# A four-part network with three batches in flight: biases added by TensorE, x*sigmoid(x) as one ScalarE function, the last step of the norms and several copies on ScalarE, queries and keys turned together

## The reference, cut to what matters

```python
# block 1: state space model (16 states), then gated attention in chunks of 256 tokens
v  = silu(xn @ v_w.T + v_b);  mx = silu(s6(xn) + xn * D_p)
u, zr, hx = split(mx @ mx_w.T + mx_b)
u = sigmoid(u);  z, r = split(silu(zr))
q, k = z * gamma0 + beta0, z * gamma1 + beta1
h = silu(hx + (softmax(q @ k.T + bias + mask) @ v * r) @ h_w.T + h_b)
out = residual + u * (h - residual)
# block 2: silu(x @ wg.T) * (x @ wu.T) @ wd.T, hidden width 384
# block 3: causal attention, 16 heads of 8, biases on q, k, v and the output
# block 4: two layers of: shift tokens, q, k, v of 8 heads of 64, q and k to unit length,
#   scale, rotate (cos, sin); attention in windows of 64; x += o @ wo;
#   layernorm over features, * ln_g + ln_b; x += (a * gelu(g)) @ w2 + b2, hidden width 341
```

## Time and profile before

| | |
|---|---|
| median of 3 runs | 1905.69 us |
| the profiled execution | 1899.97 us |
| its span | 1898.2 us (1.8 us lie around it) |
| mean granted TensorE clock | 0.895 of full |
| busy: PE, DVE, ACT, POOL | 81%, 78%, 57%, 20% of the span |
| loads of a function table | 86 |

### The profile page before, as it was taken

The page is one execution under the profiler, slowest core; times in us unless marked ns, Lnnn a source line. Parts: engine busy times, 40 slices in busy tenths (PEclk is TensorE's granted clock), DMA queues, the critical chain, the costliest instruction groups (busy, mean ns, idle before and its releaser), DMA issues.

```text
span 1898.2 us, 30428 instructions
## 1 busy us (share of the span) xinstructions
PE 1530.9 (81%) x11540; PEld 843.3 (44%) x11540; DVE 1478.0 (78%) x2885; ACT 1082.9 (57%) x2536; POOL 381.4 (20%) x279
## 2 busy tenths in 40 slices
PE   3656688889987898877778898888857888999896
PEld 1113433544544555533344455435423453465574
DVE  6999875865489978598998858898699767566855
ACT  4325515437676677635664476377642663687783
POOL 0000000303025234100321214123002112143640
PEclk7678878879999999979899899799978897999999
DMA  6651304200023200415124002232053012000110
GB/s 246 232 169 43 68 3 101 55 4 16 7 66 86 79 9 21 91 59 157 54 100 93 8 13 65 59 107 71 12 163 92 9 49 37 7 21 18 27 24 17
DMA packets 70769, 121.39 MB, mean 64 GB/s; under 512 B 6784, under 2 KB 27904, under 8 KB 68864
## 3 DMA queue, kind: packets, MB, share of 16 engines
q1 hardware_dynamic: 70624, 119.45, 22.5%
HBM read 89.14 MB, written 15.60 MB: 55 GB/s over the span
## 4 chain that ended last, share of the span: by engine, by line
PE 43%; DVE 35%; ACT 13%; issue 4%; DMA 3%; SPq 1%; POOL 1%; DVEq 0%; ACTq 0%
ACT tiles L1688 6%; DVE tiles L1130 6%; PE psum L591 5%; DVE neg_max L1284 5%; PE psum L805 4%; DVE tiles L1124 3%; DVE tiles L1134 3%; PE psum L787 2%; DVE tiles L1057 2%; PE psum L791 2%; DMA tiles<-in_ones 2%; DVE lmax L1365 2%; PE psum L764 2%; PE psum L931 2%; PE psum L940 2%
## 5 line engine op out<-in xcount | busy, mean ns | idle before, releaser
L591 PE MATMUL psum<-cst,tiles 128*128 128x128 f32 x1408 | 223.3, 296 | 111.7 <-DVE tiles L1057 72.7
L591 PEld LDWEIGHTS psum<-cst,tiles 128*128 128x128 f32 x1408 | 170.4, 151 | 192.5 <-DVE tiles L1057 69.2
L1688 ACT ACTIVATE tiles<-psum,lmax,invn 128x128 f32<-128x128 f32 x512 | 226.2, 467 | 40.4 <-DVE lmax L1370 34.5
L639 PE MATMUL psum<-tiles,cst 128*128 128x512 f32 x256 | 155.9, 741 | 65.9 <-DVE tiles L1134 65.8
L1284 DVE TENSOR_REDUCE neg_max<-psum 128x2 f32<-128x768 f32 (+3 forms) x176 | 188.2, 1120 | 21.4 <-PE psum L768 21.1
L1781 POOL TENSOR_TENSOR tiles<-tiles,lsum 128x1024 f32<-128x1024 f32 x64 | 132.3, 2068 | 291.5 <-DVE lsum L1374 291.5
L1770 POOL TENSOR_TENSOR tiles<-tiles 128x512 f32<-128x512 f32 x64 | 85.0, 1329 | 516.6 <-DVE tiles L1335 516.6
L1130 DVE TENSOR_TENSOR_SCAN tiles<-tiles 128x512 f32<-128x512 f32 x128 | 162.0, 1293 | 3.0
L1538 ACT ACTIVATE tiles<-tiles,colp 128x512 f32<-128x512 f32 x128 | 89.2, 723 | 101.7 <-DVE tiles L1130 90.7
L1622 ACT ACTIVATE tiles<-psum 128x768 f32<-128x768 f32 (+1 forms) x128 | 109.8, 922 | 39.7 <-PE psum L791 27.8
L1333 DVE TENSOR_TENSOR tiles<-psum,tables 128x512 f32<-128x512 f32 x128 | 87.5, 684 | 52.7 <-ACT tiles L1638 27.8
(11 more groups left out here) (226 smaller groups left out, 3461.0 us busy)
## 6 DMA issues: line engine op xcount, KB each, us to landing
tiles<-bc_scratch SPq DMA_DIRECT2D x128, 512.0 KB, 4.9
v_prev<-tiles SPq DMA_DIRECT2D x112, 128.0 KB, 2.4
split_scratch<-tiles SPq DMA_DIRECT2D x96, 128.0 KB, 2.4
tiles<-split_scratch SPq DMA_DIRECT2D x32, 384.0 KB
wts<-in_wts SPq DMA_DIRECT2D x1, 3114.0 KB, 15.5
tiles<-in_x SPq DMA_DIRECT2D x8, 256.0 KB, 3.0
...
```

The costliest lines, as they stand in the source:

```text
L591: ins = nc.tensor.transpose(ps[:, j * 128:(j + 1) * 128], src[:, j * 128:(j + 1) * 128], ident)
L639: ins = mm(place("y_sum", m), ident, T(S6_H[m % 3] + a), start=(m == a == 0), stop=(m == STATES // 2 - 1 and a == 1))
L1688: ins = fn(pr[:, i * 128:(i + 1) * 128], ps[:, i * 128:(i + 1) * 128], ACT.Exp, bias=own(lmax)[:, b, i:i + 1], scale=own(invn)[:, j, 0, 2 ...
```

## The change

- **Biases.** `bias_split` (POOL, once) cuts the bias rows into three bf16 parts; `biased` starts a PSUM bank with a matmul of 3 rows of ones by these parts, and the product is added to it (`v`, `u_in`, `h_out`, `v_in`, `heads_out`, `f_out`: 7 a batch). The skip term xn*D_p is one more matmul of `y_sum`, by the diagonal matrix `skip`. `ln_stats` 3 and 5 and the norms behind them read PSUM (L1239 `fo` and L1316 `aout` go).
- **Silu.** `mx`, `v_rows`, `z`, `r`, `h_silu`, `fg` are one ACTIVATE from PSUM each; the sigmoid of u is a tanh (`u_tanh`), finished in `gated`. They use another table set, `SILU`.
- **Norms.** `ln_shift` (DVE, 4 values) makes -mean*rstd, `ln_apply` (ACT, 4 instructions of 128 columns, with scale and bias per partition) applies it, in all 8 norms.
- **Copies.** `v_ext`, `o_cols`, `lpT_b` go to ACT.
- **Softplus.** `sp_exp` takes the bias in its ACTIVATEs, with one more (`Relu`) for what `sp_z` made.
- **Queries and keys.** `lqk_in` fills two banks; `qk_sq`, `qk_turned` (three instructions of twice the width) and `qk_sum` take both at once.
- **Hidden layer.** `f_centre` multiplies by I - 1/128 and gives the centred value in PSUM, so `centred` goes; ln_g is folded into `w1` once (`scaled_w1`) and ln_b into its bias (`shift_products`, `hidden_bias`), so `hgb` goes; `b2` comes by `biased`, so `y_raw` goes.
- `ORDER` and `BANKS` are new throughout (first lines of ACT's table below). On ACT the loads of a table become 128.

```diff
+DBU, HC, QK_COLS, V_EXT, O_COLS, SHIFT_B, LPT_B = "DVE", "DVE", "DVE", "ACT", "ACT", "DVE", "ACT"
+
+LN_ON_SCALAR = (0, 1, 2, 3, 4, 5, 6, 7,)
...
     "ACT": (
-        "00080010080100110100210200400310400510300600700900800a10510610710810910a00b10b20020120220420300c00d20500e00f206207209208"
+        "10080080110110210310410510610710810910a10b10c00000100200300400500610e10d00700800900a10g00b00c10f20020110i10h20200d00e203"
...
+def biased(ps, name, i=0):
+
+    prepared("fetched", "bcst")
+    pe.wait_ge(sem("bias_rows"), 32)
+    a = ROWS[name][0] + i * 128
+    mm(blocks(ps), bconst("ones", rows=PARTS), bias_parts[:, a:a + 128].unsqueeze(1).to_broadcast([PARTS, NJ, 128]),
+       start=True, stop=True, skip_group_check=True)
...
-        take("y_sum", 0, freed_by=[at("yd")])
+        prepared("skip")
+        take("y_sum", 0, freed_by=[at("mx")])
+        mm(place("y_sum", 0), skip[:, :], T(XRT), start=True, stop=False)
     for a in range(2):
-        ins = mm(place("y_sum", m), ident, T(S6_H[m % 3] + a), start=(m == a == 0), stop=(m == STATES // 2 - 1 and a == 1))
+        ins = mm(place("y_sum", m), ident, T(S6_H[m % 3] + a), start=False, stop=(m == STATES // 2 - 1 and a == 1))
...
-def lq_in(l, j):
+def lqk_in(l, j):
     lhs, a = shifted(l, j)
-    full(mm(take("lq_in", l, j, freed_by=[at("q_sq", l, j), at("q_turned", l, j)]), lhs, wts[:, a:a + 512], start=True, stop=True))
-
-def lk_in(l, j):
-    lhs, a = shifted(l, j)
-    full(mm(take("lk_in", l, j, freed_by=[at("k_sq", l, j), at("k_turned", l, j)]), lhs, wts[:, a + 512:a + 1024], start=True, stop=True))
+    ps = take("lqk_in", l, j, freed_by=[at("qk_sq", l, j), at("qk_turned", l, j)], banks=2)
+    mm(ps[:, 0:512], lhs, wts[:, a:a + 512], start=True, stop=True)
+    full(mm(ps[:, 512:1024], lhs, wts[:, a + 512:a + 1024], start=True, stop=True))
...
+def scaled_w1():
+    prepared("fetched", "wts_window")
+    dve.wait_ge(sem("products"), value[ONCE, "shift_products", ()])
+    for l in range(DEPTH):
+        w1 = wt("w1", l * 2 * HID, 2 * HID)
+        ins = ts(w1, w1, col("lg", l), None, ALU.mult)
...
+def ln_shift(k):
+    dve.wait_ge(*at("ln_rstd", k))
+    stt(out=own(shift)[:, k, :], in0=own(mv)[:, k, :, 0], scalar=-1.0, in1=own(rstd)[:, k, :], op0=ALU.mult,
+        op1=ALU.mult).then_inc(sem("ln_shift"), 1)
...
+def gated():
+    dve.wait_ge(*at("h_silu"))
+    dve.wait_ge(*normed_at(0))
+    step(tt(T(HO), T(HO), T(RES), ALU.subtract))
+    settle()
+    dve.wait_ge(*at("u_tanh"))
+    step(stt(out=T(HO), in0=T(USIG), scalar=1.0, in1=T(HO), op0=ALU.add, op1=ALU.mult))
+    settle()
+    stt(out=T(HO), in0=T(HO), scalar=0.5, in1=T(RES), op0=ALU.mult, op1=ALU.add).then_inc(sem("gated"), 1)
...
+def qk_turned(l, j):
+    prepared("tables")
+    if (l, j) > (0, 0):
+        dve.wait_ge(*product("lq_turn", *back(l, j, 1)))
+        dve.wait_ge(*product("lk_turn", *back(l, j, 1)))
+    ps = ready2("lqk_in", l, j)
+    dve.wait_ge(*at("qk_sq", l, j))
+    v = ps.rearrange("p (t h d) -> p t h d", t=2, d=LDIM)
+    cos = tables[:, l, 0:2, j, :].unsqueeze(2).to_broadcast([P, 2, LHEADS, LDIM])
+    sin = tables[:, l, 2:4, j, :].unsqueeze(2).to_broadcast([P, 2, LHEADS, LDIM])
+    t1, t2 = (T(TURNED + 2 * i, 2).rearrange("p (t h d) -> p t h d", t=2, d=LDIM) for i in range(2))
+    tt(t1, v, cos, ALU.mult)
+    tt(t2[:, :, :, 0:32], v[:, :, :, 32:64], sin[:, :, :, 0:32], ALU.mult)
+    tt(t2[:, :, :, 32:64], v[:, :, :, 0:32], sin[:, :, :, 32:64], ALU.mult).then_inc(sem("qk_turned"), 1)
...
+def f_norm(l):
+    dve.wait_ge(*at("var_rstd", l))
+    dve.wait_ge(*at("centred_sq", l))
+    tt(T(HNT), ready("f_centre", l), T(RLN), ALU.mult).then_inc(sem("f_norm"), 1)
...
+def ln_apply(k):
+    act.wait_ge(*at("ln_shift", k))
+    for j in range(NJ):
+        ins = fn(T(LN_TO[k])[:, j * 128:(j + 1) * 128], ln_in(k)[:, j * 128:(j + 1) * 128], ACT.Identity,
+                 bias=own(shift)[:, k, j:j + 1], scale=own(rstd)[:, k, j:j + 1])
+    ins.then_inc(sem("ln_apply"), 1)
...
+def sp_exp():
+    table(LNEXP)
+    prepared("fetched", "colp")
+    ps = ready("dt")
+    step(fn(T(SPE), ps, ACT.Abs, bias=col("dt_b")))
+    fn(T(SPZ), ps, ACT.Relu, bias=col("dt_b"))
+    settle()
+    fn(T(SPE), T(SPE), ACT.Exp, scale=-1.0).then_inc(sem("sp_exp"), 1)
+
+def mx():
+    table(SILU)
+    act.wait_ge(*product("y_sum", STATES // 2 - 1))
...
+def u_tanh():
+    table(SILU)
+    fn(T(USIG), ready("u_in"), ACT.Tanh, scale=0.5).then_inc(sem("u_tanh"), 1)
...
+def fg(c):
+    table(SILU)
+    fn(T(FG + c), ready("f_gate", c), ACT.Silu).then_inc(sem("fg"), 1)
...
+def qk_sum(l, j):
+    pool.wait_ge(*at("qk_turned", l, j))
+    tt(T(TURNED, 2), T(TURNED, 2), T(TURNED + 2, 2), ALU.add).then_inc(sem("qk_sum"), 1)
```

More of the change, by code:

```diff
@@ L143, in network @@
+    n += [("DVE", "ln_stats", 7), *normed(7), ("DVE", "out"), ("SP", "store")]
     return n
@@ L468, in build @@
         rstd = by_stream("rstd", [P, 8, NJ])
+        shift = by_stream("shift", [P, 8, NJ])
         rms = by_stream("rms", [P, 6, NJ])
@@ L911, in f_mean @@
                     pe.wait_ge(*at("shift2_b", l))
-                    full(mm(take("f_mean", l, freed_by=[at("centred", l)]), const("mean"), T(HT2), start=True, stop=True))
+                    full(mm(take("f_centre", l, freed_by=[at("centred_sq", l), at("f_norm", l)]), const("centre"), T(HT2), start=True, stop=True))
                 def f_var(l):
@@ L1509, in bc_rows @@
                     fn(T(BCROWS)[0:32, :], ps[0:32, :], ACT.Copy).then_inc(sem("bc_rows"), 1)
-                def sp_exp():
-                    table(LNEXP)
-                    act.wait_ge(*at("sp_z"))
-                    step(fn(T(SPE), T(SPZ), ACT.Abs))
-                    settle()
-                    fn(T(SPE), T(SPE), ACT.Exp, scale=-1.0).then_inc(sem("sp_exp"), 1)
                 def sp_ln():
@@ new lines, in v_rows, with z, r @@
+                def v_rows():
+                    table(SILU)
+                    fn(T(VAL), ready("v"), ACT.Silu).then_inc(sem("v_rows"), 1)
+                def z():
+                    prepared("fetched", "colp")
+                    table(SILU)
+                    fn(T(ZF), ready("z_in"), ACT.Silu, bias=col("bz")).then_inc(sem("z"), 1)
+                def r():
+                    prepared("fetched", "colp")
+                    table(SILU)
+                    fn(T(RF), ready("r_in"), ACT.Silu, bias=col("br")).then_inc(sem("r"), 1)
```

799 lines of the change are left out of this document (354 added, 445 removed).

## The result

| | before | changed |
|---|---|---|
| median of 8 runs each | 1908.71 us | 1920.58 us |
| lowest to highest | 1900.63 to 1914.58 | 1918.23 to 1921.39 |
| ratio, 95% interval | | 1.0062 [1.0042, 1.0082] |
| span of the profiled execution | 1898.2 us | 1919.4 us |
| mean granted TensorE clock in it | 0.895 | 0.885 |

The changed kernel is 0.6% slower; 1845 us were forecast, and the range ended at 1905. That is within the 1% which the prediction calls no change.

A forecast was written before the change was run, and what follows sets the result against it. VectorE was taken to bound the start and scans, TensorE the window attention. From 1898: -119 VectorE, +46 ScalarE, +14 TensorE, +3 GpSimd, -5 start gave a 1837 us span, 1845 us as a run; range 1765 to 1905.

The forecast's parts named there:

- the 5 that were counted: Start of S6: first `dbu` about 10 us earlier, as only one batch is prepared before it; half counted, 5 us less.
- the weight of a load of a table: ScalarE: table loads priced at ScalarE's average chain weight, 0.23 us of kernel time per busy microsecond.
- 42 x 1.283 = 54 us: ScalarE: 128 table loads for 86, the added 42 at 1.283 us each, 54 us of busy time.
- ScalarE's 200 us: ScalarE's added work: norms, copies, `Relu` and loads, less cheaper squares and overlap; at weight 0.23, 46 us slower.
- 266 x 0.45 (119): VectorE: 266 us of work removed, times its average chain weight of 0.45, 119 us faster.
- 0.53: TensorE's chain weight per busy microsecond; 27 us of added bias and skip products cost 14 us.
- 3 us for the longer sum: GpSimd: queries and keys both wait for the 1024-column `qk_sum`, 0.7 to 1.3 us later per token block; priced 3 us.
- The waits change hands: Rival, 17%: removed VectorE work stood behind remaining scans and reductions, weight 0.22; 59 us won, 60 paid, about 1900.
- ScalarE takes VectorE's place: Rival, 11%: in window attention and norms, ScalarE's weight rises from 0.23 to 0.32; 1957 us.
- ACT above 25% of the chain: Sign that the forecast is wrong: this ScalarE share, with waits of PE or DVE on `ln_apply`.
- the other sign: Sign that the forecast is wrong: VectorE's chain share unchanged at shorter busy time, its weight never in the removed work.
- PE fills up: Rival, 18%: TensorE becomes the only bound, busy 90.5% after the start; 1787 us, about 1760 with a higher clock.

The follow-up runs named there:

- a_oneset: Changed kernel in its own order with one table set for all (Silu, Tanh, Gelu, Sigmoid as Relu), 127 of 128 loads gone: 1835.55 us, ratio 0.9645.
- b_oneset: Kernel before in its own order with one table set for all (Sigmoid as Exp, Gelu as Relu), 85 of 86 loads gone: 1893.45 us, ratio 0.9947.
- a_replanned: Changed kernel, every instruction kept, its three batches interleaved anew on each engine by a search, 82 table loads instead of 128: 1875.41 us, ratio 0.9859.
- b_thin: Kernel before in its own order, part of the VectorE work the change removes cut to 4 columns for batches 3 to 7: 1883.43 us, ratio 0.9899.
- a_two_sums: Changed kernel with the rotation's sum on GpSimd as two instructions of 512 columns, queries first and waited for alone: 1910.28 us, ratio 1.0052.
- a_norms_vector: Changed kernel in its own order with the last step of the eight norms back on VectorE: 1926.34 us, ratio 1.0127.
- a_scalar_order: Changed kernel with only ScalarE's row interleaved anew by the search, PSUM banks reassigned, 89 table loads instead of 128: 1866.76 us, ratio 0.9796.

## Why the prediction was wrong

- **The busy times** were nearly right: DVE 1242 (1190 to 1235 forecast, 7 us outside; 236 us came off instead of 266), ACT 1285.8 (1250 to 1320), PE 1586.7 (1520 to 1590), 128 loads of 1.283 us. `ln_apply` has a mean of 0.46 to 0.49 us, but four in a row take 1.62 us, 0.40 each. The first `dbu` started at 38.0 us instead of 41.1, not at 31; that is 3 us of the 5 that were counted.
- **The step that failed is the weight of a load of a table.** The prediction wrote "42 x 1.283 = 54 us" into ScalarE's 200 us and multiplied all by 0.23: 12 us. It took it that the 86 loads already there stay as cheap as they were. They didn't: all 128 cost 79 us (a_oneset), the 86 of before 10 us (b_oneset). The price of the loads went up by some 69 us where 12 were counted, and the place decides it: the new order puts single gates and decay factors of different batches between loads, while 81 loads in the order of a_replanned cost 8 us. That the instruction behind a load is ready (113 of 128) is part of it but not the whole, as the 62 of 86 before show; what makes a ready instruction one that others wait for was not measured load by load. An average over an engine mixes work that stands in its waits with work that pushes others, and the order decides which is which.
- **A second step was mis-sized:** "266 x 0.45 (119)". For a third of the work taken away b_thin gives 0.26 [0.19 to 0.33]; carried over to all 236 us that is 61, between 45 and 78. The prediction had this as a rival with 0.22, and named why: of the lines that go, only L1057 was on the chain.
- **TensorE:** the weight is right (0.56 for 0.53), the bias and skip instructions cost 19 us instead of 14. PE's busy time rose by 56 us and not 27; 34 are these instructions, and without loads PE, with every instruction kept, is busy for 25 us less (a_oneset). So the rest belongs to the price of the loads.
- **GpSimd:** 3 us for the longer sum; none shown by a_two_sums.
- **The rivals.** "The waits change hands" (about 1900) came nearest in time, and its half weight is right, but its other half, 60 us paid, was paid otherwise. "ScalarE takes VectorE's place" named the engine and, among its reasons, a load in front of the norm; its place, the norms, is refuted by a_norms_vector. Its sign was ACT above 25% of the chain: ACT has 15 of the 60% that can be followed, a quarter, so the sign stood at its edge and did not decide. DVE has 11 of 60 after 35%, so the other sign, its share unchanged, was not met, though its weight in the work taken away was too high all the same. "PE fills up" is far off: PE rose from 81 to 83%.
- **The Trainium skill's rules.** By "What ACT_TABLE_LOAD costs" (ScalarE: Activation LUTs, 2.66 us a switch) the loads would have been dearer than the trace shows, with a drain of 1.38 us. The traces still show none: load ends at 794.56, next start 794.57. Even 2.66 us would not have given the right answer at a weight of 0.23 (26 us). What would have helped is the Trainium skill's rule in "Table sets: the hidden batching unit" (ScalarE: Activation LUTs): group calls by set, not by function. a_scalar_order, with 39 loads less, agrees in direction. The prediction's other rule would have left the norms on VectorE, "by a fifth" (1.62 us of ScalarE for 1.28 of VectorE, a quarter); a_norms_vector shows that 12 us slower in this order.
- **The account.** The prediction's terms without its 12 us for loads add up to 73 us less; a_oneset against b_oneset measures 58 less. Its 12 us for loads measure 69. So of the 73 us by which the forecast missed, 57 are the loads and 16 all the rest, with some 6 us of uncertainty on each. The rest does not split so well: -61 (VectorE) + 19 (TensorE) - 3 (start) is -45, without the other 149 us of ScalarE's new work, against the 58 measured. VectorE's term alone is uncertain by 17 us, b_thin measured five of eight batches in before's order, and two orders are compared. So norms and copies on ScalarE cost little here, or the order won their cost back; which of the two was not separated.
